# Six residual additions of a gated recurrent layer moved into accumulating transfers

## The chip, the cores and the metric

The kernel runs on one core of one Trainium2 chip. The metric is device microseconds of one execution. The kernel before took 118.81 us in the median of three runs (118.44 to 119.31). The execution under the profiler took 118.47 us, 0.34 us under that median.

## The reference, cut to what matters

```python
# inputs x: (16 sequences, 512 steps, 128 features), float32
xn = layernorm(x)
r, k, v = split(xn @ W_rkv + b_rkv, 3);  r = sigmoid(r);  k = exp(k);  kv = k * v
gamma = exp(nu_log + gamma_log) - 1;     lam = exp(-exp(nu_log))
u1, u2 = scan(lam, kv), scan(lam, k)          # y[t] = lam * y[t-1] + u[t] along the 512 steps
s = ((u1 + gamma * kv) / (u2 + gamma * k + 1e-6) * r) @ W_o + b_o
g = silu(fp6_quantised(xn) @ fp6_quantised(W_ffn).T + bias)   # blocks of 32, one scale each
out = x + s * g
```

The last line is the residual addition that the change is about.

## The kernel before, in words

A sequence is one tile of 128 partitions x 512 float32 elements (256 KB); there are 16, and all of them stay in `x_all`. Every sequence goes through the same stages, spread over the engines:

- VectorE: `statistics` of the layer norm, `block_maxima` and scales of the quantisation, `key_values` (k times v), the two scans `scan_den` and `scan_num`, `receive` (numerator times receptance), `gating` (projection times gate).
- GpSimd: a quarter of `normalise`, `quantise`, `dequantise`, `gamma_k`, `denominator` and `ratio` (the last six mostly for two sequences at once).
- ScalarE: three quarters of `normalise`, the copies of the turned tiles out of PSUM, exponential, tanh, silu, the logarithm and its inverse for the division, and the seven pairs of table loads between the set of exp and log and the set of silu and tanh (`exp_phase`, `silu_phase`).
- TensorE: transposes of `xn` and `xd`, the matmuls `keys`, `receptance`, `values`, `ffn`, `project`, and `untranspose` of the gated product.

The term gamma times kv of the numerator is added by TensorE (`gamma_kv`, a matmul with a diagonal matrix that accumulates in `num_ps`) for the eight even sequences, and by VectorE for the eight odd ones. The residual of sequence n is added in one of two ways. For the 12 sequences of `RES_DVE`, VectorE adds `x_all` and the PSUM bank `so_ps` into `x_all`. For the four of `RES_POOL`, 2, 5, 8 and 11, ScalarE copies the bank to one of two buffers `product` (`copy_out`, line 824), and GpSimd adds that to `x_all` (line 390). SyncE then stores `x_all[:, n, :]` to the output, 16 stores in order of sequence. `project(n + 1)` uses the same PSUM bank `so_ps` up to sequence 12, so it waits until the residual or the copy of n has read it.

The order of the work is written out by hand, one list for each engine, and each engine runs its list in order and stops at a semaphore that has not come. Two more lists, `TURNS` and `TAKEN`, give the order in which two pairs of PSUM banks are used: `turned_ps` (transposes, emptied by ScalarE's copies) and `taken_ps` (keys, receptance and ffn, emptied by ScalarE's exp, tanh and silu). The use i of a pair waits until use i - 2 has been emptied. `project(15)` takes the bank `taken_ps[0]` after all 48 uses, so it waits for `gates(15)` on ScalarE.

SyncE issues the 16 loads of x and the three weight loads first, and then the stores.

Of the kernel before, what the change touches and what calls it, by code (L numbers as in the profile page):

```python
# [5 lines left out]
def build(nc, x_in, w_rkv, b_rkv, w_o, b_o, nu_log, gamma_log, w_ffn, b_ffn, out):  # L6
# [10 lines left out]
    SEQS, L, D = x_in.shape  # L17
# [30 lines left out]
    def batch_of(batches, n):  # L48
# [3 lines left out]
    RES_POOL = [2, 5, 8, 11]  # L52
    RES_DVE = [n for n in range(SEQS) if n not in RES_POOL]
    STORES = [0, 1, 2, 3, 4, 5, 6, 7, 8, 9, 10, 11, 12, 13, 14, 15]
# [27 lines left out]
    with ctx:  # L82
# [34 lines left out]
        product = sb("product", [P, 2, W])  # L117
# [107 lines left out]
        pool_result = sem("pool_result")  # L225
# [43 lines left out]
        def _(sp):  # L269
# [10 lines left out]
            for n in range(4, SEQS):  # L280
                load(n)
            for n in STORES:
                if n in RES_POOL:
                    sp.wait_ge(pool_result, RES_POOL.index(n) + 1)
                else:
                    sp.wait_ge(dve_result, RES_DVE.index(n) + 1)
                sp.dma_start(out_v[:, n, :], x_all[:, n, :]).then_inc(stored, 16)
            sp.wait_ge(stored, SEQS * 16)

        @block.gpsimd  # L290
        def _(pool):
# [108 lines left out]
            normalise(2)  # L400
            dequantise(0)
            deviations(3)
            normalise(3)
            inv_std(3)
            quantise(1)
            gamma_k(0)
            normalise(4)
            denominator(0)
            gamma_k(1)
            dequantise(1)  # L410
            normalise(5)
            denominator(1)
            quantise(2, 2)
            dequantise(2, 2)
            normalise(6)
            deviations(4)
            ratio(0)
            normalise(7)
            inv_std(4)
            gamma_k(2, 2)  # L420
            quantise(4, 2)
            ratio(1)
            normalise(8)
            dequantise(4, 2)
            gamma_k(4, 2)
            denominator(2, 2)
            normalise(9)
            quantise(6, 2)
            normalise(10)
            denominator(4, 2)  # L430
            ratio(2, 2)
            deviations(5)
            dequantise(6, 2)
            inv_std(5)
            gamma_k(6, 2)
            residual(2)
            normalise(11)
            quantise(8, 2)
            ratio(4, 2)
            normalise(12)  # L440
            denominator(6, 2)
            dequantise(8, 2)
            normalise(13)
            quantise(10, 2)
            dequantise(10, 2)
            normalise(14)
            gamma_k(8, 2)
            ratio(6, 2)
            gamma_k(10, 2)
            residual(5)  # L450
            denominator(8, 2)
            denominator(10, 2)
            normalise(15)
            quantise(12, 2)
            ratio(8, 2)
            dequantise(12, 2)
            gamma_k(12, 2)
# [6 lines left out]
            gamma_k(14)  # L464
            gamma_k(15)
            denominator(14)
            denominator(15)
            dequantise(15)
            ratio(12, 2)
            ratio(14)  # L470
            ratio(15)
            residual(11)

        @block.vector
        def _(dve):
# [125 lines left out]
            out_weights()  # L601
            statistics(4)
            block_scales(0)
            inverse_scales(0)
            statistics(5)
            statistics(6)
            statistics(7)
            decay_column()
            key_values(0)
            scan_den(0)  # L610
            ffn_weights()
            block_maxima(1)
            gamma()
            block_scales(1)
            inverse_scales(1)
            scan_num(0)
            key_values(1)
            statistics(8)
            block_maxima(2)
            statistics(9)  # L620
            scan_den(1)
            block_scales(2)
            inverse_scales(2)
            block_maxima(3)
            key_values(2)
            statistics(10)
            receive(0)
            statistics(11)
            scan_num(1)
            block_scales(3)  # L630
            inverse_scales(3)
            gamma_kv(1)
            key_values(3)
            receive(1)
            scan_den(2)
            scan_num(2)
            gating(0)
            key_values(4)
            scan_den(3)
            residual(0)  # L640
            statistics(12)
            key_values(5)
            receive(2)
            block_maxima(4)
            statistics(13)
            statistics(14)
            scan_num(3)
            block_scales(4)
            inverse_scales(4)
            gamma_kv(3)  # L650
            gating(1)
            scan_den(4)
            scan_den(5)
            receive(3)
            key_values(6)
            residual(1)
            scan_num(4)
            statistics(15)
            key_values(7)
            block_maxima(5)  # L660
            receive(4)
            block_scales(5)
            inverse_scales(5)
            key_values(8)
            gating(2)
            scan_num(5)
            scan_den(6)
            gamma_kv(5)
            scan_den(7)
            gating(3)  # L670
            receive(5)
            key_values(9)
            scan_num(6)
            residual(3)
            block_maxima(6)
            receive(6)
            gating(4)
            scan_num(7)
            residual(4)
            block_scales(6)  # L680
            inverse_scales(6)
            gamma_kv(7)
            scan_den(8)
            scan_den(9)
# [3 lines left out]
            gating(5)  # L688
            block_maxima(7)
            receive(8)  # L690
            scan_den(10)
            scan_num(9)
            scan_den(11)
            gating(6)
            gamma_kv(9)
            key_values(11)
            receive(9)
            residual(6)
            scan_num(10)
            block_scales(7)  # L700
            inverse_scales(7)
            gating(7)
            scan_den(12)
            scan_den(13)
            key_values(12)
            residual(7)
            block_maxima(8)
            receive(10)
            gating(8)
            scan_num(11)  # L710
            block_scales(8)
            inverse_scales(8)
            gamma_kv(11)
            scan_den(14)
# [3 lines left out]
            key_values(13)  # L718
            scan_den(15)
            receive(12)  # L720
            residual(9)
            scan_num(13)
            key_values(14)
            gating(10)
            gamma_kv(13)
            receive(13)
            residual(10)
            scan_num(14)
            key_values(15)
            gating(11)  # L730
            receive(14)
            scan_num(15)
            gamma_kv(15)
            receive(15)
            gating(12)
            gating(13)
            gating(14)
            residual(12)
# [6 lines left out]
        def _(act):  # L745
# [510 lines left out]
```

## Time and profile before

| | |
|---|---|
| profiled execution | 118.47 us, span of the core 116.7 us |
| TensorE (PE) busy | 107.5 us, 92% of the span |
| VectorE (DVE) busy | 105.6 us, 91% |
| ScalarE (ACT) busy | 101.7 us, 87% |
| GpSimd (POOL) busy | 100.8 us, 86% |
| DMA | 8.81 MB, mean 76 GB/s |

A share is busy time over the span. The span holds a head in which the first tiles are loaded and normalised, and a tail of the last residual and its store, so no engine can reach 100%. Outside the span lie 1.77 us of the execution. Matmuls overlap their neighbours: the time from one to the next, in the chain of work, is shorter than the mean duration of one.

### The profile page before, as it was taken

Reading aid. Unit: us, or ns where it says so; the run is one execution under the profiler, and the core shown is the slowest. Engines: PE = TensorE matmul, PEld = TensorE weight load, DVE = VectorE, ACT = ScalarE, POOL = GpSimd, SP = SyncE. Lnnn points to the kernel's source line nnn. Section 1 sums busy time; section 2 is a strip of 40 time slices with the busy share of each in tenths; the row PEclk is TensorE's granted clock in tenths of the full one; section 3 lists DMA queues with packets and bytes.
Section 4 is the critical chain, followed back from the end, with each engine's and each line's share of the span. In section 5 each row is a group of like instructions: output and inputs, shape, how many; then the busy total and the mean of one; then the engine's idle time right before and its main releaser. Section 6 shows DMA issues by size and latency. Waiting matters only on the chain.

```text
span 116.7 us, 1669 instructions
## 1 busy us (share of the span) xinstructions
PE 107.5 (92%) x403; PEld 59.1 (51%) x403; DVE 105.6 (91%) x171; ACT 101.7 (87%) x176; POOL 100.8 (86%) x110
## 2 busy tenths in 40 slices
PE   4947999979999999999999999999999999999970
PEld 4934435535455546445473544755545554545550
DVE  0539999999999999999998999999999899999891
ACT  4049899999999999999999999999998999899700
POOL 2189978999999999798999999999999999997800
PEclk9999999999999999999999999999999999999996
DMA  2869960000002000200022100021111021020047
GB/s 70 244 199 404 386 248 0 0 6 3 6 0 90 0 0 0 90 0 0 18 77 90 65 25 0 0 89 43 53 41 54 0 90 72 18 90 0 0 184 265
DMA packets 6024, 8.81 MB, mean 76 GB/s; under 512 B 1536, under 2 KB 1920, under 8 KB 6016
## 3 DMA queue, kind: packets, MB, share of 16 engines
q1 hardware_dynamic: 5040, 8.72, 20.7%
q10 hardware_dynamic: 976, 0.00, 0.5%
q8 instruction: 3, 0.05, 0.2%
q14 instruction: 5, 0.04, 0.1%
HBM read 4.53 MB, written 4.19 MB: 75 GB/s over the span
## 4 chain that ended last, share of the span: by engine, by line
PE 74%; ACT 12%; DVE 3%; DMA 3%; POOL 3%; issue 1%; DVEq 1%; ACTq 0%; POOLq 0%
PE taken_ps L1020 32%; PE turned_ps L1001 11%; PE so_ps L1076 10%; PE v_ps L1048 10%; PE num_ps L1062 5%; PE so_ps L1082 5%; ACT xn L764 5%; DMA x_all<-in_L_attn_inputs_dram 3%; ACT L747 2%; POOL rstd L316 2%; ACT k L792 2%; ACT recept L799 2%; DVE x_all L553 2%; PE turned_ps L1076 1%; DVE gate L548 1%
## 5 line engine op out<-in xcount | busy, mean ns | idle before, releaser
L1020 PE MATMUL taken_ps<-xnT,wrkv_sb 128*128 128x512 f32 x64 | 31.8, 597 | 0.3 <-ACT k L792 0.3
L764 ACT ACTIVATE xn<-x_all,shift,rstd 128x128 f32<-128x128 f32 x48 | 20.1, 497 | 5.7 <-POOL shift L336 5.7
L384 POOL TENSOR_TENSOR mixed<-mixed,den 128x1024 f32<-128x1024 f32 (+1 forms) x10 | 19.3, 1934 | 2.0 <-ACT den L817 1.2
L527 DVE TENSOR_TENSOR_SCAN num_ps<-own_ps,kv 128x512 f32<-128x512 f32 x16 | 19.4, 1215 | 0.0
L378 POOL TENSOR_TENSOR den<-den,gk 128x1024 f32<-128x1024 f32 (+1 forms) x10 | 19.2, 1930 | 0.1
L517 DVE TENSOR_TENSOR_SCAN den<-own_ps,k 128x512 f32<-128x512 f32 x16 | 19.1, 1207 | 0.0
L747 ACT ACT_TABLE_LOAD x14 | 18.0, 1283 | 0.9 <-PEq L1243 0.7
L481 DVE BATCH_NORM_STATS2 stats<-x_all 128x6 f32<-128x256 f32 x32 | 11.7, 417 | 6.2 <-DMA x_all<-in_L_attn_inputs_dram 6.2
L1048 PE MATMUL v_ps<-xnT,wrkv_sb 128*128 128x512 f32 x32 | 16.4, 595 | 0.0
L1020 PE MATMUL taken_ps<-xdT,wdT 128*128 128x512 f32 x32 | 16.2, 599 | 0.1
L355 POOL TENSOR_TENSOR q<-xn,inv_scale 128x1024 fp8e4<-128x1024 f32 (+1 forms) x10 | 15.7, 1571 | 0.4 <-DVE inv_scale L500 0.4
L362 POOL TENSOR_TENSOR xd<-q,scale 128x1024 f32<-128x1024 fp8e4 (+1 forms) x10 | 15.7, 1568 | 0.3
L1020 PEld LDWEIGHTS taken_ps<-xnT,wrkv_sb 128*128 128x128 f32 x64 | 11.0, 190 | 9.5 <-issue 8.7
L1076 PE MATMUL so_ps<-mixed,wos_sb 128*128 128x512 f32 x26 | 13.8, 611 | 0.0
L1001 PEld LDWEIGHTS turned_ps<-ident,xn 128*128 128x128 f32 x64 | 7.5, 141 | 12.0 <-issue 9.6
L1001 PE MATMUL turned_ps<-ident,xn 128*128 128x128 f32 x64 | 9.8, 276 | 3.7 <-POOL xn L347 2.3
L508 DVE SCALAR_TENSOR_TENSOR kv<-v_ps,cols,k 128x512 f32<-128x512 f32 x16 | 11.7, 731 | 0.1
L807 ACT ACTIVATE gate<-taken_ps,cols 128x512 f32<-128x512 f32 x16 | 10.9, 695 | 0.6 <-PE taken_ps L1020 0.5
L792 ACT ACTIVATE k<-taken_ps,cols 128x512 f32<-128x512 f32 x16 | 10.9, 692 | 0.5 <-PE taken_ps L1020 0.4
L542 DVE SCALAR_TENSOR_TENSOR mixed<-recept,num_ps 128x512 f32<-128x512 f32 x16 | 10.8, 674 | 0.1
L799 ACT ACTIVATE recept<-taken_ps,half_br 128x512 f32<-128x512 f32 x16 | 10.8, 692 | 0.0
L548 DVE SCALAR_TENSOR_TENSOR gate<-so_ps,cols,gate 128x512 f32<-128x512 f32 x13 | 9.6, 741 | 1.1 <-ACT recept L799 0.5
(73 smaller groups left out, 188.2 us busy)
## 6 DMA issues: line engine op xcount, KB each, us to landing
x_all<-in_L_attn_inputs_dram SPq DMA_DIRECT2D x16, 256.0 KB, 6.6
out_dram<-x_all SPq DMA_DIRECT2D x16, 256.0 KB, 2.0
wrkv_sb<-in_L_attn_W_rkv_dram SPq DMA_DIRECT2D x1, 192.0 KB, 4.4
wf_sb<-in_L_ffn_weight_dram SPq DMA_DIRECT2D x1, 64.0 KB, 6.3
wo_sb<-in_L_attn_W_o_dram SPq DMA_DIRECT2D x1, 64.0 KB, 6.1
cols<-in_L_attn_nu_log_dram ACTq DMA_DIRECT2D x1, 0.5 KB, 3.8
cols<-in_L_attn_gamma_log_dram ACTq DMA_DIRECT2D x1, 0.5 KB, 4.0
cols<-in_L_attn_b_o_dram ACTq DMA_DIRECT2D x1, 0.5 KB, 4.6
```

The lines of the kernel that those rows point to most:

```text
L355: nc.gpsimd.tensor_tensor(blocks(ring(q, n, m)), blocks(ring(xn, n, m)), spread(iscale(n, m)), ALU.mult, saturate=False).then_inc(q_ready, m)
L362: nc.gpsimd.tensor_tensor(blocks(ring(xd, n, m)), blocks(ring(q, n, m)), spread(scale[:, n * BPS:(n + m) * BPS]), ALU.mult).then_inc(xd_re ...
L378: nc.gpsimd.tensor_tensor(ring(den, n, m), ring(den, n, m), ring(gk, n, m), ALU.add)\
L384: nc.gpsimd.tensor_tensor(ring(mixed, n, m), ring(mixed, n, m), ring(den, n, m), ALU.mult)\
L517: nc.vector.tensor_tensor_scan(den[:, n % DEN, :], lam_ps.to_broadcast([P, W]), k[:, n % KS, :], 0.0, ALU.mult, ALU.add).then_inc(den_scan ...
L527: nc.vector.tensor_tensor_scan(num_ps[:, :], lam_ps.to_broadcast([P, W]), kv[:, n % KS, :], 0.0, ALU.mult, ALU.add).then_inc(num_scanned, 1)
L747: act.add_instruction(mybir.InstLoadActFuncSet(name=nc.get_next_instruction_name(), engine=mybir.EngineType.Activation, act_func_set_id=n, ...
L764: ins = nc.scalar.activation(xn[:, n % XN, j * D:(j + 1) * D], x_all[:, n, j * D:(j + 1) * D], ACT.Identity, bias=shift[:, t:t + 1], scale ...
L1001: ins = nc.tensor.transpose(in_time(turned_ps[i % 2][:, :])[:, :, j], source[:, j * D:(j + 1) * D], ident[:, :])
L1020: nc.tensor.matmul(taken_ps[i % 2][:, :], weights, moving, start=True, stop=True).then_inc(filled, 1)
L1048: nc.tensor.matmul(v_ps[:, :], wrkv_sb[:, 2 * D:3 * D], xnT[:, n % XNT, :], start=True, stop=True)\
L1076: nc.tensor.matmul(SO_BANKS[n][:, :], wos_sb[:, :], mixed[:, n % MIX, :], start=True, stop=True)\
```

## The change

`RES_POOL` grows from four sequences to six: 2, 4, 6, 8, 10 and 12. Their rows of x are stored to the output before any residual (`placed`), by SyncE behind the loads. GpSimd no longer adds in SBUF: its `residual(n)` issues a transfer that adds `product` to the output in HBM. `product` has four buffers instead of two. `gamma_kv` goes to TensorE for ten sequences (0, 1, 3, 4, 6, 8, 10, 12, 14, 15) and stays on VectorE for six (2, 5, 7, 9, 11, 13). The lists of all engines are written out in a new order.

```diff
-    RES_POOL = [2, 5, 8, 11]
+    RES_POOL = [2, 4, 6, 8, 10, 12]
+    PRODUCTS = 4
     TURNS = [
-        ("xn", 0), ("xn", 1), ("xn", 2), ("xn", 3), ("xd", 0), ("xn", 4), ("xn", 5), ("xd", 1), ("xd", 2),
+        ("xn", 0), ("xn", 1), ("xn", 2), ("xd", 0), ("xn", 3), ("xn", 4), ("xn", 5), ("xd", 1), ("xd", 2),
...
-        product = sb("product", [P, 2, W])
+        product = sb("product", [P, PRODUCTS, W])
...
-        pool_result = sem("pool_result")
+        placed = {n: sem(f"placed{n}") for n in RES_POOL}
+        added = [sem(f"added{i}") for i in range(len(RES_POOL))]
...
             for n in range(4, SEQS):
                 load(n)
+            for n in RES_POOL:
+                sp.wait_ge(x_loaded[n], 16)
+                sp.dma_start(out_v[:, n, :], x_all[:, n, :]).then_inc(placed[n], 16)
             for n in STORES:
                 if n in RES_POOL:
-                    sp.wait_ge(pool_result, RES_POOL.index(n) + 1)
-                else:
-                    sp.wait_ge(dve_result, RES_DVE.index(n) + 1)
+                    continue
+                sp.wait_ge(dve_result, RES_DVE.index(n) + 1)
                 sp.dma_start(out_v[:, n, :], x_all[:, n, :]).then_inc(stored, 16)
-            sp.wait_ge(stored, SEQS * 16)
+            sp.wait_ge(stored, len(RES_DVE) * 16)
+            for done in added:
+                sp.wait_ge(done, 16)
...
             def residual(n):      # GpSimd
                 i = RES_POOL.index(n)
                 pool.wait_ge(copied_out, i + 1)
-                nc.gpsimd.tensor_tensor(x_all[:, n, :], x_all[:, n, :], product[:, i % 2, :], ALU.add)\
-                    .then_inc(pool_result, 1)
+                pool.wait_ge(placed[n], 16)
+                nc.gpsimd.dma_start(out_v[:, n, :], product[:, i % PRODUCTS, :], accum_op=ALU.add)\
+                    .then_inc(added[i], 16)
...
             def copy_out(n):      # ScalarE
                 i = RES_POOL.index(n)
                 act.wait_ge(o_done, n + 1)
-                if i >= 2:
-                    act.wait_ge(pool_result, i - 1)
-                nc.scalar.activation(product[:, i % 2, :], so_ps[:, :], ACT.Copy).then_inc(copied_out, 1)
+                if i >= PRODUCTS:
+                    act.wait_ge(added[i - PRODUCTS], 16)
+                nc.scalar.activation(product[:, i % PRODUCTS, :], so_ps[:, :], ACT.Copy).then_inc(copied_out, 1)
```

The new order at the start of TensorE's list, against the old one:

```
before: xn0 xn1 k0 v0 k1 xn2 arm r0 r1 v1 xn3 r2 xd0 v2 xn4 wd gkv0 k2 k3 xn5 v3 k4 k5 xd1 xd2 ffn0 r3 p0 v4 r4
        gkv2 un0 v5 xn6 ffn1 xn7 r5 xd3 p1
after:  xn0 xn1 k0 v0 k1 xn2 arm xd0 r0 v1 xn3 r1 gkv0 r2 k2 xn4 xn5 v2 k3 gkv1 k4 xd1 v3 k5 xd2 wd v4 p0
        ffn0 ffn1 v5 xd3 r3 un0 xn6 r4 p1
```

(xn, xd and wd are transposes, k, r, v, ffn and p the matmuls `keys`, `receptance`, `values`, `ffn` and `project`, gkv is `gamma_kv`, un is `untranspose`.) At the end, TensorE's list has `project(12)`, `gamma_kv(15)`, `project(13)`, `ffn(15)`, `untranspose(12)`, `project(14)`, `project(15)`, `untranspose(13)` to `untranspose(15)`. VectorE's ends with the gatings 13 to 15 and the residuals 13, 14 and 15; before, `residual(12)` stood ahead of `gating(15)`. ScalarE's list ends with `gates(14)`, `gates(15)` and `copy_out(12)`; the other five copies stand ahead of these, where before there were four.

## Rows read from the trace of the kernel before

**Rows 1.** The page: busy time of each engine, and the chain that ended last, by engine.
```profile
PE 107.5 (92%) x403; PEld 59.1 (51%) x403; DVE 105.6 (91%) x171; ACT 101.7 (87%) x176; POOL 100.8 (86%) x110
PE 74%; ACT 12%; DVE 3%; DMA 3%; POOL 3%; issue 1%; DVEq 1%; ACTq 0%; POOLq 0%
```

**Rows 2.** Busy time by stretch: stretch, its length, PE, PEld, DVE, ACT, POOL, clock, DMA share, GB/s.
```profile
9.00:25.00 16.00, 14.13 (x49) 6.82 (x49) 15.61 (x41) 15.44 (x34) 14.57 (x26) 1.00 0.49 184
25.00:110.00 85.00, 84.57 (x305) 44.58 (x306) 83.28 (x118) 83.49 (x139) 81.24 (x70) 1.00 0.09 35
```

**Rows 3.** The chain that ended last, in order of time: start us, us, what.
```profile
0.72 3.61 DMA x_all<-in_L_attn_inputs_dram
...
15.08 0.48 ACT xnT L773
...
25.06 0.63 PE turned_ps L1001 x4
...
33.83 0.86 PE num_ps L1062 x2
34.69 0.47 PE so_ps L1082 x4
...
36.02 0.44 PE turned_ps L1001 x4
...
39.06 0.86 PE so_ps L1076 x2
...
108.34 1.73 PE turned_ps L1076 x4
...
111.55 0.75 DVE gate L548
112.30 1.20 DVE x_all L553 x2
```

**Rows 4.** Waits, all engines: who waited for whom, us in total, times, longest.
```profile
PE turned_ps L1001 <- ACT xdT L780: 0.8, 1, 0.8
```

**Rows 5.** Groups of instructions, forms apart, of the lines that the change touches.
```profile
L1062 PE MATMUL num_ps<-kv,gam_diag 128*128 128x512 f32 x16 | 8.2, 593 | 0.0
L533 DVE SCALAR_TENSOR_TENSOR num_ps<-kv,gam,num_ps 128x512 f32<-128x512 f32 x8 | 5.7, 708 | 0.0
L553 DVE TENSOR_TENSOR x_all<-so_ps,x_all 128x512 f32<-128x512 f32 x9 | 6.1, 677 | 0.0
L390 POOL TENSOR_TENSOR x_all<-x_all,product 128x512 f32<-128x512 f32 x4 | 5.1, 1284 | 0.0
L824 ACT ACTIVATE product<-so_ps 128x512 f32<-128x512 f32 x4 | 2.4, 594 | 0.5 <-PE so_ps L1082 0.5
```

**Rows 6.** The same view: groups that bound the cost of an issue on GpSimd.
```profile
L384 POOL TENSOR_TENSOR mixed<-mixed,den 128x1024 f32<-128x1024 f32 x6 | 14.2, 2373 | 0.9 <-ACT den L817 0.6 <-issue 0.2
L316 POOL TENSOR_TENSOR rstd<-var,minus_half 128x4 f32<-128x4 f32 x2 | 2.0, 1024 | 0.0
L500 DVE RECIPROCAL inv_scale<-scale 128x32 f32<-128x32 f32 x7 | 2.5, 353 | 0.2
```

**Rows 7.** Timeline of the ramp: start us, us, engine, line, instruction, count.
```profile
13.29 0.75 DVE L508 SCALAR_TENSOR_TENSOR kv<-v_ps,cols,k 128x512 f32<-128x512 f32 x1
13.73 1.05 POOL L362 TENSOR_TENSOR xd<-q,scale 128x512 f32<-128x512 fp8e4 x1
17.56 1.02 PE L1048 MATMUL v_ps<-xnT,wrkv_sb 128*128 128x512 f32 x2
22.44 1.28 ACT L747 ACT_TABLE_LOAD   x1
26.70 1.91 POOL L362 TENSOR_TENSOR xd<-q,scale 128x1024 f32<-128x1024 fp8e4 x1
```

**Rows 8.** SyncE's queue: the last loads, the stores by line, and their time to landing.
```profile
4.00 6.80 SPq L271 DMA_DIRECT2D x_all<-in_L_attn_inputs_dram  x12
L287 SPq DMA_DIRECT2D out_dram<-x_all x16: 332/332/347, 36.1 to 114.1; - x16
out_dram<-x_all SPq DMA_DIRECT2D x16, 256.0 KB, 2.0
```

**Rows 9.** Timeline of the tail.
```profile
108.93 1.27 ACT L807 ACTIVATE gate<-taken_ps,cols 128x512 f32<-128x512 f32 x2
109.70 1.29 POOL L390 TENSOR_TENSOR x_all<-x_all,product 128x512 f32<-128x512 f32 x1
110.37 1.07 PE L1076 MATMUL taken_ps<-mixed,wos_sb 128*128 128x512 f32 x2
```

More of the change, by code:

```diff
@@ L400, in _ @@
             normalise(2)
+            normalise(3)
+            deviations(3)
             dequantise(0)
-            deviations(3)
-            normalise(3)
+            gamma_k(0)
+            gamma_k(1)
             inv_std(3)
             quantise(1)
-            gamma_k(0)
+            denominator(0)
             normalise(4)
-            denominator(0)
-            gamma_k(1)
+            normalise(5)
             dequantise(1)
-            normalise(5)
-            denominator(1)
             quantise(2, 2)
-            dequantise(2, 2)
             normalise(6)
             deviations(4)
+            denominator(1)
+            dequantise(2, 2)
             ratio(0)
+            inv_std(4)
+            quantise(4, 2)
             normalise(7)
-            inv_std(4)
-            gamma_k(2, 2)
-            quantise(4, 2)
             ratio(1)
@@ L428, in _ @@
             quantise(6, 2)
+            dequantise(6, 2)
             normalise(10)
             denominator(4, 2)
+            gamma_k(6, 2)
+            normalise(11)
+            deviations(5)
             ratio(2, 2)
-            deviations(5)
-            dequantise(6, 2)
             inv_std(5)
-            gamma_k(6, 2)
+            quantise(8, 2)
+            gamma_k(8, 2)
             residual(2)
-            normalise(11)
-            quantise(8, 2)
-            ratio(4, 2)
             normalise(12)
             denominator(6, 2)
+            normalise(13)
+            ratio(4, 2)
             dequantise(8, 2)
-            normalise(13)
+            denominator(8, 2)
             quantise(10, 2)
-            dequantise(10, 2)
[L446 to L451, printed above, removed]
+            residual(4)
+            normalise(14)
+            normalise(15)
+            gamma_k(10, 2)
+            ratio(6, 2)
+            dequantise(10, 2)
             denominator(10, 2)
-            normalise(15)
+            gamma_k(12, 2)
+            residual(6)
+            ratio(8, 2)
             quantise(12, 2)
-            ratio(8, 2)
             dequantise(12, 2)
-            gamma_k(12, 2)
             denominator(12, 2)
@@ L464, in _ @@
             gamma_k(14)
+            dequantise(15)
             gamma_k(15)
+            residual(10)
             denominator(14)
+            ratio(12, 2)
             denominator(15)
-            dequantise(15)
-            ratio(12, 2)
             ratio(14)
             ratio(15)
-            residual(11)
+            residual(12)
         @block.vector
@@ L641, in _ @@
+            block_maxima(4)
+            gating(1)
+            gamma_kv(2)
             statistics(12)
-            key_values(5)
             receive(2)
-            block_maxima(4)
+            residual(1)
+            block_scales(4)
+            inverse_scales(4)
+            scan_num(3)
+            scan_den(4)
+            key_values(6)
+            scan_den(5)
+            receive(3)
+            key_values(7)
+            scan_num(4)
             statistics(13)
             statistics(14)
-            scan_num(3)
@@ L648, in _ @@
[L648 to L657, printed above, removed]
             statistics(15)
-            key_values(7)
+            key_values(8)
+            receive(4)
             block_maxima(5)
-            receive(4)
+            scan_num(5)
             block_scales(5)
             inverse_scales(5)
-            key_values(8)
+            gamma_kv(5)
@@ L992, in _ @@
             gates(15)
+            copy_out(12)
         @block.tensor
@@ L1111, in _ @@
-            values(3)
-            keys(4)
-            keys(5)
-            transpose_xd(1)
-            transpose_xd(2)
+            keys(3)
+            gamma_kv(1)
+            keys(4)
+            transpose_xd(1)
+            values(3)
+            keys(5)
+            transpose_xd(2)
+            transpose_wd()
+            values(4)
+            project(0)
             ffn(0)
+            ffn(1)
+            values(5)
+            transpose_xd(3)
             receptance(3)
-            project(0)
@@ L1119, in _ @@
-            values(4)
+            untranspose(0)
+            transpose_xn(6)
             receptance(4)
-            gamma_kv(2)
-            untranspose(0)
-            values(5)
-            transpose_xn(6)
-            ffn(1)
+            project(1)
             transpose_xn(7)
             receptance(5)
-            transpose_xd(3)
-            project(1)
-            transpose_xn(8)
-            ffn(2)
-            ffn(3)
-            values(6)
-            transpose_xn(9)
-            keys(6)
@@ L1136, in _ @@
-            keys(7)
+            receptance(6)
             untranspose(1)
             transpose_xd(4)
+            keys(6)
+            values(6)
+            transpose_xd(5)
+            keys(7)
+            transpose_xn(8)
+            gamma_kv(3)
+            values(7)
+            transpose_xn(9)
             keys(8)
-            values(7)
+            transpose_xd(6)
             keys(9)
+            values(8)
             gamma_kv(4)
-            transpose_xd(5)
-            values(8)
+            ffn(2)
@@ L1158, in _ @@
             transpose_xn(11)
             gamma_kv(6)
-            project(4)
             ffn(6)
             transpose_xn(12)
-            untranspose(4)
+            receptance(10)
+            project(4)
+            transpose_xn(13)
             keys(10)
```

295 lines of the change are left out of this document (145 added, 150 removed), and 12 rows, old and new, of tables (TAKEN, TURNS).

## The prediction

> **What bounds the kernel now.** I read the busy shares first, then the chain that ended last, then the stretches. The shares alone don't decide: four engines stand between 86% and 92% [rows 1]. The chain does. It lies on TensorE for 74% of the span [rows 1], and in order of time it stays there from the transpose at 25.06 us to the end of `project(14)` at 108.34 + 1.73 = 110.07 us [rows 3]. The stretch 25 to 110 us says how close the others come: of 85.0 us TensorE is busy 84.6, ScalarE 83.5, VectorE 83.3 and GpSimd 81.2 [rows 2]. So GpSimd has 3.8 us to spare there and no other engine more than 1.7; TensorE ends last, but nobody is far behind it.
>
> TensorE's busy time hides a little waiting, since a matmul's record is longer than its step. Its steps in the chain are 0.86 us for a matmul of 512 columns in its two passes, 0.44 for four transposes of xn or xd, 0.47 for an untranspose [rows 3]. Between 25.06 and 110.07 us its list has 76 such matmuls, 26 transposed tiles and 12 untransposed ones: 65.4 + 11.4 + 5.6 = 82.4 us of 85.0. So 2.6 us of waits are left in it.
>
> The tail is tied to two engines. `gates(15)` ends at 108.93 + 1.27 = 110.20 us, and `project(15)`, which needs its bank, starts at 110.37 [rows 9]; then come its gating, its untranspose, the residuals 14 and 15 and a store of 2.0 us [rows 3, 8].
>
> **The change part by part.**
>
> *TensorE* gets two more `gamma_kv`, at 0.86 us from one to the next [rows 3]; the 593 ns of a pass overlap [rows 5]. That is +1.72 us on the engine that is the chain. What could cover it is its 2.6 us of waits and the ramp.
>
> *The ramp.* Before, `xn5` waits 0.8 us for ScalarE to copy xd0, whose bank it takes over [rows 4]; it starts at 25.06 [rows 3]. In the new `TURNS`, xd0 comes ahead of xn3, so xn4 and xn5 take over banks long empty. I walk the four new lists by hand with the steps of the old trace, and note where TensorE would stop. xd0 on GpSimd moves behind a normalise and two small instructions, from 13.73 to 14.8, so its 1.05 us end near 15.85 [rows 7]; TensorE waits some 0.5 us for it. The product kv of sequence 0 on VectorE (13.29 before [rows 7]) moves behind block maxima, gamma and scales to about 15.4, and values(1) is then due at 17.2, against 17.56 before [rows 7]. xn4 and xn5 follow at 21.9 and 22.3, keys(3) ends at 24.5, gamma_kv(1) at 25.5 behind its scan. xd2 waits about 0.5 us for a dequantise on GpSimd which, at 26.70 before [rows 7], now stands behind a quantise, a normalise, the deviations and a denominator and ends near 29.0. `project(0)` is then due at 30.5 and `project(1)` at 36.95 to 37.8. Before, project(1) ended at 39.06 + 0.86 = 39.92 [rows 3]. The new list has by then left out receptance(5) and one transpose, 0.86 + 0.44 = 1.3 us: equal work is done at 39.1, so TensorE is 0.8 us ahead, both extra `gamma_kv` not yet paid in full. (gamma_kv(2) of before is matched by gamma_kv(1); the two extra ones come later, 3 beside 4, and 15.) On the same walk ScalarE is not ahead: its table load at 22.44 [rows 7] moves 0.48 later for the copy of xd0 that now stands ahead of it.
>
> *ScalarE* gets two more copies out. A copy is 594 ns alone and 0.48 from start to start in a row [rows 3, 5]. One lies ahead of `gates(15)`: +0.5 us with 0.1 from the ramp, +0.6. The other lies after it, covered by the tail's work on TensorE and VectorE. ScalarE has 1.5 us free [rows 2], so this is less than TensorE's term and beside it.
>
> *VectorE* loses two `gamma_kv` and two residuals: 2 x 708 + 2 x 677 ns = 2.8 us [rows 5]. It isn't the chain before the tail, so nothing of that comes off the sum directly. In the tail `residual(12)` no longer stands ahead of `gating(15)`, but that one waited for project(15) just as long (110.37 + 1.07 = 111.44 against a start at 111.55 [rows 3, 9]): -0.1.
>
> *GpSimd* loses four additions, 5.1 us in all [rows 5], 4.1 of them ahead of 110 us, since the last starts at 109.70 [rows 9]. It gets six issues, five of them ahead of 110 us. The trace has no transfer issued by GpSimd. The cost c of an issue is bounded below by SyncE's issue of the same tile, 0.33 us [rows 8], and above by the longest instruction that GpSimd runs, 2.37 [rows 6]. I take 1.0: this is software on GpSimd over few operands, and the nearest row is the power of 4 elements per partition, 1.02 us though it moves almost nothing [rows 6]. Then GpSimd's stretch is 81.2 - 4.1 + 5.0 = 82.1 us of 85: almost no relief, no harm. Range: 78.8 to 89.0.
>
> The Trainium skill, DMA: Bandwidth & Descriptors, section Latency and other measured facts, puts the first byte of a GpSimd-issued transfer at about 1 us and lays it on the descriptors being written by its cores; as an estimate of c that leaves the sum where it is, and no run here shows it yet. One of its rules speaks against the change: by SBUF — State Buffer, section Who interferes with whom, VectorE in a two-port mode locks GpSimd out of writing descriptors. VectorE's small SBUF-only instructions here last up to 353 ns [rows 6], so by that rule six issues would cost at most 2.1 us more, on an engine with 2.9 us left.
>
> Queued behind each issue on GpSimd are the next quantise, ratio or normalise, for whom TensorE and ScalarE wait; that is how c would show. Its wait for `placed` costs nothing: the stores ahead go out behind the loads.
>
> *SyncE* issues six more stores at 0.33 us [rows 8]. They wait for x behind the last load's issue at 4.00 + 6.80 = 10.8 us [rows 8], in the same queue as the loads, and the first ordinary store is at 36.1 [rows 8]. So I cost them at nothing: the queue's order keeps them behind the loads, and DMA is 9% busy after 25 us [rows 2]. Without that cover, 1.5 MB at the ramp's 184 GB/s [rows 2] would be 8 us of DMA, and the statistics of the last sequences would be late next.
>
> *Sum:* +1.72 - 0.8 - 0.1 = +0.8 us on a span of 116.7, so 117.5, and 119.3 us for that execution (118.47 before). The median stands 0.34 us above the profiled one (118.81), so I forecast 119.6 us.
>
> **The rivals.**
>
> *A, the relief closes TensorE's waits.* VectorE is 2.8 us freer, and GpSimd too if c is near its lower bound. If TensorE's 2.6 us of waits came from them being late, the re-ordered lists could take these away: +0.8 - 2.6 = -1.8, span 114.9, time 117.0; with a little of it left, 117.2. For it: both are within 4 us of full, and the buffers are short. Against: ScalarE is as full and gets more work, so it can't go far under +0.6 less its own 1.5 us of idle, -0.9, unless its records too hide waits, as TensorE's do.
>
> *B, GpSimd becomes the bound (slower).* Its place is the stretch 25 to 110 us. 81.2 - 4.1 + 5c passes 85 from c = 1.6 on, if GpSimd never waits. At c = 2.0 it is 87.1; with half of its former idle time, 1.9, kept, 89.0. That is +2.1 to +4.0 us, about +3.1: 121.9 us. For it: GpSimd does everything in software (1.28 us for a tile that VectorE adds in 0.68 [rows 5]). Against: an issue touches no elements.
>
> *C, the last accumulating transfer lands last.* copy_out(12) ends near 110.2 + 0.6 = 110.8, the issue at 111.8, both 0.8 later with the shift. Landing is bounded by a store, 2.0 us [rows 8], and by a read and a store, 3.6 + 2.0 = 5.6 [rows 3, 8], as it must read the output first; I take 3.5. SyncE's last store goes out at 114.1 and lands at 116.1 [rows 8], so the transfer decides from a landing of 4.3 us on. At 5.6 it adds 1.3: 120.9 us.
>
> *D, the change doesn't relieve anybody.* If c is about 1.28, the issue costs what the addition did. That is inside the forecast: +0.8 either way.
>
> **How the numbers follow.** What a measurement can tell from no change is about 1%, 1.2 us: under 117.6 is faster, over 120.0 slower. The forecast gets 0.45, from 118.9 to 120.5; 0.35 of this lies within 1%, 0.10 over it. A gets 0.29, 0.25 of it faster. B gets 0.18, 0.16 of it slower. C gets 0.08, half and half between within and slower. That makes faster 0.25, within 0.45, slower 0.30. The range goes from A at 117.2 to B at 121.9 us; outside are A with every wait gone, and c near 2.37.
>
> **What would show it.** TensorE: the wait for xdT at 25 us gone, project(1) ending at 37.8, and the chain on TensorE from about 25 to 111 us. GpSimd: the gap around each residual's issue gives c; under 0.6 speaks for A, over 1.6 for B. The tail: last landing by SyncE's store of 15, else C. ScalarE starting `gates(15)` before 109.5 would refute my sum, and so would waits on GpSimd's issues as the cause of idle TensorE; a chain that leaves TensorE for ScalarE or VectorE in the middle of the span would mean that the two extra matmuls were not the price.

## The result and the profile after

The changed kernel took 121.75 us in the median of four runs (121.68 to 122.1), beside 118.66 us for the kernel before (118.44 to 119.31). The ratio is 1.026, with a 95% interval of 1.023 to 1.030: 3.1 us slower. The forecast was 119.6 us and no measurable change. The time lies inside the range of 117.2 to 121.9 us only because that range was wide; it comes near the 121.9 us of rival B, and not for that rival's reason, as the experiments show.

The changed kernel's page, with busy time by engine and the chain that ended last by engine, answers to [rows 1]:

```profile
PE 109.7 (92%) x407; PEld 60.1 (50%) x407; DVE 106.3 (89%) x167; ACT 102.9 (86%) x178; POOL 101.1 (84%) x112
PE 69%; DVE 17%; DMA 5%; issue 4%; SPq 1%; DVEq 1%
```

VectorE lost two `gamma_kv` and two residuals, four instructions in all, and yet it is busy 0.7 us longer; and it holds 17% of the chain where it held 3%. Its busy time by stretch, in the columns of [rows 2]:

```profile
9.00:25.00 16.00, 14.58 (x53) 7.41 (x54) 15.75 (x40) 15.36 (x33) 14.92 (x27) 1.00 0.75 282
25.00:110.00 85.00, 83.67 (x302) 43.58 (x301) 83.44 (x115) 82.18 (x139) 80.12 (x70) 1.00 0.17 38
```

TensorE, nearly full before (84.57 of 85.00), is idle for 1.3 us here. The chain in order of time says where: it runs on VectorE up to 31.3 us, and on TensorE from there (before, from 25.06).

```profile
25.88 0.65 DVE kv L518
26.52 0.20 DVE wmax L586
26.73 0.02 issue
26.75 0.59 DVE wscale L589
...
27.58 1.75 DVE wq L594
...
30.53 0.75 DVE kv L518
31.28 0.14 issue
31.41 1.10 PE v_ps L1056 x2
...
39.04 0.86 PE so_ps L1084 x2
```

The span is cut at two matmuls of `project`: `project(1)`, the last row above, at 39.04 us in the chain (39.06 before [rows 3]), and `project(15)`, at 112.53 in the rows below (110.37 before [rows 9]). A timeline gives the same `project(1)` a start 0.17 us earlier than the chain does, 38.87 and 38.89, so the two measures are not mixed below. The changed kernel's tail, by TensorE, GpSimd and SyncE's queue:

```profile
112.53 1.09 PE L1084 MATMUL taken_ps<-mixed,wos_sb 128*128 128x512 f32 x2
...
113.17 0.88 POOL L398 DMA_DIRECT2D out_dram<-product  x1 [1.37 <-ACT product L830]
...
115.10 1.53 SPq L292 DMA_DIRECT2D out_dram<-x_all  x3
```

| stretch | before | after | difference |
|---|---|---|---|
| to `project(1)`; the new list has then left out 1.3 us of TensorE's work | 39.06 | 39.04 (and 1.3) | +1.3 |
| `project(1)` to `project(15)`, less that 1.3 | 71.3 | 73.5 - 1.3 | +0.9 |
| `project(15)` to the end of the span | 6.3 | 7.3 | +0.9 |

The sum is the 3.1 us between the spans, 116.7 and 119.8.

How the transfers themselves look is seen in two rows on the line that issues them, and in the DMA part of the page:

```profile
L398 POOL DMA_DIRECT2D out_dram<-product x6: 877/884/1145, 60.0 to 113.2; - x6
DMA to landing us min/median/max: 3.7/4.0/4.4
```

```profile
out_dram<-x_all SPq DMA_DIRECT2D x16, 256.0 KB, 3.1
out_dram<-product POOLq DMA_DIRECT2D x6, 256.0 KB, 4.0
```

The 3.1 us is a median over three kinds of store: the six beforehand, beside the loads (7.4 us in the median), the seven of the body (2.0), and the last three, which are the matter of the tail below (3.1).

An issue is recorded with 0.88 us. GpSimd's timeline shows that less than that is lost, since the next instruction starts before the record ends:

```profile
92.91 0.88 POOL L398 DMA_DIRECT2D out_dram<-product  x1
93.52 1.35 POOL L362 TENSOR_TENSOR q<-xn,inv_scale 128x512 fp8e4<-128x512 f32 x1
```

From start to start it is 0.61 us here. The other four ahead of the last have 0.64, 0.64, 0.67 and 0.85. An addition in SBUF had 1.24 (75.90 to 77.14 us in the trace of before).

GpSimd's busy time misleads here. Behind the first issue most of its other records are some 0.3 us longer and overlap the next one, though the steps are the old ones:

```profile
61.28 2.66 POOL L385 TENSOR_TENSOR den<-den,gk 128x1024 f32<-128x1024 f32 x1
63.64 0.72 POOL L354 TENSOR_SCALAR xn<-x_all,rstd,shift 128x128 f32<-128x128 f32 x1
```

The denominator is recorded with 2.66 us (2.37 before), but the next instruction starts 2.36 us after it.

### The profile page after: what moved, and what is told of

Its sections match the earlier page's. It is cut to its first block, busy times and chain, and to the rows that moved or that the text cites. A ratio compares the mean times of both kernels' runs of the same rounds, so it can differ in the third digit from the quotient of the medians.

```text
span 119.8 us, 1686 instructions
## 1 busy us (share of the span) xinstructions
PE 109.7 (92%) x407; PEld 60.1 (50%) x407; DVE 106.3 (89%) x167; ACT 102.9 (86%) x178; POOL 101.1 (84%) x112
## 4 chain that ended last, share of the span: by engine, by line
PE 69%; DVE 17%; DMA 5%; issue 4%; SPq 1%; DVEq 1%
PE taken_ps L1028 28%; PE so_ps L1084 10%; PE v_ps L1056 9%; PE turned_ps L1009 8%; PE num_ps L1070 6%; PE so_ps L1090 5%; DMA x_all<-in_L_attn_inputs_dram 5%; DVE stats L491 5%; DVE own_ps L498 2%; DVE den L527 2%; DVE kv L518 2%; DVE wq L594 1%; PE turned_ps L1084 1%; DVE num_ps L537 1%; SPq L273 1%
## 5 line engine op out<-in xcount | busy, mean ns | idle before, releaser
L391 POOL TENSOR_TENSOR mixed<-mixed,den 128x1024 f32<-128x1024 f32 (+1 forms) x10 | 20.8, 2080 | 1.0 <-DVE mixed L552 0.6
L385 POOL TENSOR_TENSOR den<-den,gk 128x1024 f32<-128x1024 f32 (+1 forms) x10 | 20.7, 2070 | 0.1
L362 POOL TENSOR_TENSOR q<-xn,inv_scale 128x1024 fp8e4<-128x1024 f32 (+1 forms) x10 | 16.5, 1646 | 1.8 <-issue 1.8
L369 POOL TENSOR_TENSOR xd<-q,scale 128x1024 f32<-128x1024 fp8e4 (+1 forms) x10 | 16.8, 1677 | 0.3
L1009 PEld LDWEIGHTS turned_ps<-ident,xd 128*128 128x128 f32 x64 | 7.7, 142 | 6.3 <-issue 4.2
```

Of the source, the lines that this page charges most:

```text
L369: nc.gpsimd.tensor_tensor(blocks(ring(xd, n, m)), blocks(ring(q, n, m)), spread(scale[:, n * BPS:(n + m) * BPS]), ALU.mult).then_inc(xd_re ...
L385: nc.gpsimd.tensor_tensor(ring(den, n, m), ring(den, n, m), ring(gk, n, m), ALU.add)\
L391: nc.gpsimd.tensor_tensor(ring(mixed, n, m), ring(mixed, n, m), ring(den, n, m), ALU.mult)\
L1009: ins = nc.tensor.transpose(in_time(turned_ps[i % 2][:, :])[:, :, j], source[:, j * D:(j + 1) * D], ident[:, :])
```

## The experiments

Medians differ by some tenths between the chips, so each kernel is compared by its ratio to the kernel before on the same chip; a difference of 0.001 in a ratio is about 0.12 us.

**The ffn weight's scales in PSUM.** On the chain above stand instructions of a group of five small ones that quantise the ffn weight: a maximum, a scale (`wscale`), its reciprocal, and two products (`wq`, `wd`). Side by side, VectorE and GpSimd of the changed kernel between 25 and 31 us:

```profile
26.75 0.58 DVE L589 TENSOR_SCALAR wscale<-wmax 128x4 f32<-128x4 f32 x1
27.37 0.18 DVE L592 RECIPROCAL wiscale<-wscale 128x4 f32<-128x4 f32 x1
27.58 1.74 DVE L594 TENSOR_TENSOR wq<-wf_sb,wiscale 128x128 fp8e4<-128x128 f32 x1
29.36 1.25 DVE L597 TENSOR_TENSOR wd<-wq,wscale 128x128 f32<-128x128 fp8e4 x1
...
26.03 1.28 POOL L385 TENSOR_TENSOR den<-den,gk 128x512 f32<-128x512 f32 x1
27.27 1.91 POOL L369 TENSOR_TENSOR xd<-q,scale 128x1024 f32<-128x1024 fp8e4 x1
29.14 1.32 POOL L391 TENSOR_TENSOR mixed<-mixed,den 128x512 f32<-128x512 f32 x1
```

The ends are what to look at: 27.33 against 27.31, 29.32 against 29.18, 30.61 against 30.46. Each of the three ends just after the GpSimd instruction that was running. The reciprocal, which runs inside GpSimd's dequantise as well, keeps its 0.18 us. In the kernel before, the same work stood beside GpSimd instructions of 0.2 to 0.5 us:

```profile
15.39 0.17 DVE L579 TENSOR_SCALAR wscale<-wmax 128x4 f32<-128x4 f32 x1
15.81 0.29 DVE L584 TENSOR_TENSOR wq<-wf_sb,wiscale 128x128 fp8e4<-128x128 f32 x1
16.13 0.29 DVE L587 TENSOR_TENSOR wd<-wq,wscale 128x128 f32<-128x128 fp8e4 x1
```

The edit takes no work away. It moves the input and the output of wscale and of the reciprocal, and one input of each product, from SBUF to PSUM:

```diff
-        wmax = sb("wmax", [P, BPW])
-        wscale = sb("wscale", [P, BPW])
-        wiscale = sb("wiscale", [P, BPW])
+        wmax, wscale, wiscale = (own_ps[:, at:at + BPW] for at in (400, 408, 416))
```

> The changed kernel with one edit: the three small columns of the ffn weight's quantisation (wmax, wscale, wiscale) lie in a free part of the PSUM bank own_ps instead of SBUF, so VectorE's five instructions on that weight read SBUF through at most one operand. No list is reordered. Theory P (port collision): in the changed kernel wscale, wq and wd take 0.58, 1.74 and 1.25 us instead of 0.17, 0.29 and 0.29, and each ends within 0.1 us of the end of a GpSimd instruction; with one operand in PSUM they take under 0.5 us each, kv of sequence 3 comes about 2.5 us earlier, project(0) starts near 30.5 instead of 32.35, and the time falls by about 1.9 us, from 121.75 to 119.9 us (ratio to before 1.010). Rival O (order alone): the chain is late because of where it stands in the list, the long records are its waits; then the time stays at 121.4 to 121.8 us (ratio 1.024).

Measured: 119.92 us, ratio 1.011 (1.006 to 1.016). VectorE's timeline of that kernel, the same instructions in the same place, while the same GpSimd product runs (27.20 to 29.12 us):

```profile
26.69 0.17 DVE L587 TENSOR_SCALAR own_ps<-own_ps 128x4 f32<-128x4 f32 x1
26.90 0.19 DVE L590 RECIPROCAL own_ps<-own_ps 128x4 f32<-128x4 f32 x1
27.12 0.29 DVE L592 TENSOR_TENSOR wq<-wf_sb,own_ps 128x128 fp8e4<-128x128 f32 x1
27.45 0.29 DVE L595 TENSOR_TENSOR wd<-wq,own_ps 128x128 f32<-128x128 fp8e4 x1
```

and TensorE's `project(1)`:

```profile
37.13 1.02 PE L1082 MATMUL so_ps<-mixed,wos_sb 128*128 128x512 f32 x2
```

The stretch is gone and 1.8 us of the 3.1 are back. `project(1)` starts 1.74 us earlier than in the changed kernel; in the chain's measure, which the prediction's walk used, it is at 37.30 us where the walk had 36.95. The order was mostly not what failed; the durations were. The new order also moves the scaling of the output weight, from 10.05 to 24.10 us. It takes 0.65 us there instead of 0.21 and ends 0.09 us after a quantise on GpSimd; here, with input and output still in SBUF, it takes 0.49.

**One part of the new order in the kernel before.** The same weight work moved late in the old lists, with the scales in SBUF and then in PSUM.

```diff
 # VectorE                          # TensorE                     # ScalarE
             scan_den(0)
-            ffn_weights()
...
             key_values(2)
+            ffn_weights()
...
             transpose_xd(2)
+            transpose_wd()         # was ahead of gamma_kv(0)
...
             keys(5)
             inverse(1)
+            copy_wdT()             # was behind keys(3)
```

> The kernel before with one part of the new order alone: VectorE quantises the ffn weight behind key_values(2), near 25.4 us, where GpSimd runs additions and products of two operands in SBUF, instead of near 15 us, where it runs small ones. The transpose of the weight and its copy move behind transpose_xd(2) and inverse(1). Theory P (port collision): wscale, wq and wd together take at least 1.5 us more than the 0.75 us they take before, and the kernel gets 1 to 2 us slower, 119.5 to 120.5 us (ratio 1.009 to 1.017). Rival O (order alone): the five instructions keep their 1.3 us in all, 118.3 to 118.9 us.

> e8_before_late_weights, with wmax, wscale and wiscale in PSUM as in e1. The same order of work, without a second SBUF operand on VectorE. Theory P: no stretched instruction, 118.3 to 118.9 us (ratio 0.998 to 1.003). Rival O: the same as e8, whatever that is.

Measured: 122.05 us, ratio 1.024 (1.017 to 1.032) with the scales in SBUF; 119.78 us, ratio 1.006 (1.002 to 1.011) in PSUM. The first is slower than expected, the second slightly too, so the late place costs 0.7 us by itself and the collision 2.2 us on top. In the first, by VectorE and then GpSimd:

```profile
25.24 0.89 DVE L579 TENSOR_SCALAR wscale<-wmax 128x4 f32<-128x4 f32 x1
26.16 0.18 DVE L582 RECIPROCAL wiscale<-wscale 128x4 f32<-128x4 f32 x1
26.38 1.93 DVE L584 TENSOR_TENSOR wq<-wf_sb,wiscale 128x128 fp8e4<-128x128 f32 x1
...
24.19 1.91 POOL L355 TENSOR_TENSOR q<-xn,inv_scale 128x1024 fp8e4<-128x1024 f32 x1
26.25 1.91 POOL L362 TENSOR_TENSOR xd<-q,scale 128x1024 f32<-128x1024 fp8e4 x1
```

wscale (4 elements per partition) ends at 26.13, GpSimd's quantise at 26.10; wq ends at 28.31, the dequantise at 28.16. The reciprocal again takes its 0.18 us. This is the collision made in a kernel that had none.

**The weights early, in SBUF.** The practical way round: back to a place where GpSimd runs small instructions.

```diff
             block_maxima(0)
+            out_weights()
...
             scan_den(0)
+            ffn_weights()
             statistics(9)
```

> The changed kernel with VectorE's two pieces of weight work back near their old places, and still in SBUF: out_weights behind block_maxima(0), ffn_weights behind scan_den(0), near 17.2 us, where GpSimd runs only small instructions. Theory P: the five instructions take about 1.3 us in all, scan_num(0) and gamma_kv(0) come 1.3 us later and cost TensorE up to 0.9 us there, the 2.3 us of waits at 28.5 to 31.4 go: 1.0 to 1.9 us less than the changed kernel, ratio 1.011 to 1.018. Rival O (what counts is not the port but something else behind the weights in the list): 1.022 or over.

Measured: 120.97 us, ratio 1.017 (1.013 to 1.021), the slow end of the expectation. wscale, wq and wd take 0.22, 0.29 and 0.29 us. `scan_num(0)` comes later, and TensorE waits 0.95 us for it ahead of `gamma_kv(0)`, at 20.56 us. By the ratios this brings 1.1 us where the scales in PSUM brought 1.8, and `project(1)` starts 1.2 us later than with these: the place costs some of what it avoids.

**The tail.** The last accumulating transfer, of sequence 12, is issued at 113.17 us. It has landed before the last store, at 117.5, but its packets, 0.18 us each for 2 KB where a store's take 0.09, move until 117.15. The last three stores are issued from 115.10 on, and their first packet starts 1.4 us later, where a store alone has 0.8. The last of them is issued at 116.30 and waited for until 119.4: 3.1 us, against 2.2 before. Two edits on top of the scales in PSUM: the residual of 12 given to VectorE, and, in a second kernel, given to GpSimd as an addition in SBUF.

```diff
 # given to VectorE
-    RES_POOL = [2, 4, 6, 8, 10, 12]
+    RES_POOL = [2, 4, 6, 8, 10]
...
             gating(14)
+            residual(12)
             gating(15)
 # or added in SBUF by GpSimd, stored ahead of 13
+                if n == RES_POOL[-1]:
+                    nc.gpsimd.tensor_tensor(x_all[:, n, :], x_all[:, n, :], product[:, i % PRODUCTS, :], ALU.add)\
+                        .then_inc(last_added, 1)
+                    return
```

> e1_psum_scales with one more edit: the residual of sequence 12 is added by VectorE again (ahead of gating 15, as before) and stored by SyncE; five accumulating transfers are left. Theory L (the accumulating transfer of 12 runs beside the last three stores and stretches the last one: 3.1 us from issue to the end of SyncE's wait instead of 2.2): the stretch from project(15) to the end falls from 7.1 to about 6.3 us, so 119.1 us (ratio 1.003), against 119.9 for e1. Rival N (that stretch is longer for another reason, such as the longer list of semaphores at the end, or VectorE's extra residual takes it back): 119.7 us or more.

> e1_psum_scales with the residual of sequence 12 added in SBUF by GpSimd and stored by SyncE ahead of 13; the other five stay accumulating transfers, no list of a compute engine is changed and VectorE gets nothing more. Theory L (the accumulating transfer in the tail stretches the last stores): from project(15) to the end 6.3 to 6.5 us as in the kernel before, instead of 7.1, so 0.6 to 0.8 us less than e1, ratio to before 1.004 (e1: 1.011). Rival N (the tail is longer for the semaphores that SyncE waits on, or for another reason): the same tail and time as e1, ratio 1.010.

Measured: 120.01 us, ratio 1.009 (1.005 to 1.012) for the first; 119.49 us, ratio 1.004 (1.001 to 1.007) for the second, as forecast. In the second, `project(15)` starts at 111.79 and the span ends at 118.2: 6.4 us, as before. SyncE's queue and the landings of that kernel:

```profile
113.53 2.37 SPq L294 DMA_DIRECT2D out_dram<-x_all  x4
```

```profile
out_dram<-x_all SPq DMA_DIRECT2D x16, 256.0 KB, 2.1
```

The last store takes 2.2 us again. So theory L holds, worth 0.7 us in the trace (a tail of 7.1 us with the scales alone, 6.4 here) and 0.8 by the ratios (1.011 to 1.004), whose intervals just overlap. The first edit brought 0.2 us at most, which its interval cannot tell from nothing: VectorE's extra residual stands ahead of `gating(15)`, and the load of TensorE's weights for `untranspose(15)` waits 0.5 us for that gating.

**The mechanism alone.** The kernel before, its lists untouched, with the four residuals sent as accumulating transfers.

```diff
-                nc.gpsimd.tensor_tensor(x_all[:, n, :], x_all[:, n, :], product[:, i % 2, :], ALU.add)\
-                    .then_inc(pool_result, 1)
+                pool.wait_ge(placed[n], 16)
+                nc.gpsimd.dma_start(out_v[:, n, :], product[:, i, :], accum_op=ALU.add).then_inc(added[i], 16)
```

> The kernel before with the mechanism alone: residuals 2, 5, 8 and 11 go out as accumulating transfers onto x stored beforehand, four product buffers; no list is reordered and VectorE keeps its twelve residuals. Theory M: an issue holds GpSimd for 0.61 to 0.85 us from its start to the next instruction, against 1.24 for the addition, so GpSimd gains 4 x 0.6 = 2.4 us, but TensorE is the chain; the last transfer is issued near 109.7 and lands near 114.5, ahead of the last store. So 118.2 to 118.9 us (ratio 0.996 to 1.002). Rival R (the relief is what TensorE waits for): 117.5 us or less. Rival C (accumulating transfers are slow and are waited for): 119.5 us or more.

Measured: 119.05 us, ratio 1.004 (1.001 to 1.008), just over the band of theory M; the profiled execution has the span of before, 116.7. By stretch, the kernel before and then this one (40 to 110 us):

```profile
40.00:110.00 70.00, 69.63 (x251) 36.73 (x250) 68.32 (x93) 68.61 (x109) 66.94 (x53) 1.00 0.10 38
```

```profile
40.00:110.00 70.00, 69.69 (x252) 36.74 (x250) 68.32 (x93) 68.52 (x108) 65.90 (x53) 1.00 0.16 38
```

GpSimd is 1.0 us less busy (66.94 to 65.90), and from start to start three issues take 2.2 us where three additions took 3.7; TensorE gains nothing. Rival A's reading of GpSimd's relief is refuted for this order of work. The last three stores take 2.4 us here against 2.1, which may be the excess over the band; that was not tried apart.

**The mechanism taken out of the changed kernel.** Six additions in SBUF, everything else as changed.

```diff
-                pool.wait_ge(placed[n], 16)
-                nc.gpsimd.dma_start(out_v[:, n, :], product[:, i % PRODUCTS, :], accum_op=ALU.add)\
-                    .then_inc(added[i], 16)
+                nc.gpsimd.tensor_tensor(x_all[:, n, :], x_all[:, n, :], product[:, i % PRODUCTS, :], ALU.add)\
+                    .then_inc(pool_result, 1)
```

> The changed kernel, its lists and its six sequences, but the residuals are added in SBUF by GpSimd again and stored by SyncE; no stores beforehand, four product buffers kept. GpSimd gets 6 x 0.6 = 3.6 us more, the tail loses the late accumulating transfer (0.7 us of waiting at the end in the changed kernel). If GpSimd has that much room: 121.0 us (ratio 1.020). If GpSimd becomes the bound: 122.5 us or more (ratio over 1.032), and then the transfers do bring something in this order of work.

Measured: 121.44 us, ratio 1.025 (1.019 to 1.030), the same as with the transfers. From project(1) to project(15) it takes 113.51 - 39.77 = 73.74 us by the timeline, against 112.53 - 38.87 = 73.66 with transfers. So the transfers neither cost nor bring anything in the body of this kernel, and rival B is refuted: five additions take 2.8 us more there than the five issues, and GpSimd is still not the bound. The tail is no shorter, 7.0 us: this kernel stores 12 behind 13 and 14, right ahead of 15, and the last store takes 2.6 us beside them. The stores beforehand are gone here too, so this does not tell them from the transfers.

**`gamma_kv` given back to VectorE.** Three kernels were tried: 3 and 15 in the changed kernel; 12, behind scan_den(14), on top of the edits of scales and residual 12; and 12 behind residual(9), on top of the last addition in SBUF.

```diff
 # VectorE (and the same calls taken from TensorE's list)
             scan_num(3)
+            gamma_kv(3)
...
             gating(12)
+            gamma_kv(15)
 # second kernel                     # third kernel
             scan_den(14)                         residual(9)
+            gamma_kv(12)             +            gamma_kv(12)
             residual(9)                          scan_den(15)
```

> The changed kernel with gamma_kv 3 and 15 taken from TensorE and given to VectorE, as eight and eight stood before; nothing else. Theory T (TensorE is the rigid chain after the ramp): two matmuls of 0.86 us less, so 1.2 to 1.7 us faster, 120.0 to 120.5 us (ratio 1.011 to 1.016). Rival V (VectorE is as close): its 2 x 0.6 us more eat the gain, 121.3 us or more (ratio over 1.022).

> e5_scales_res12 with gamma_kv 12 moved from TensorE to VectorE, behind scan_den(14), in the stretch where VectorE idles 1.4 of 20 us. If TensorE is the rigid chain once no list starves it: 0.86 us less than e5, 118.2 us (ratio 0.996). If VectorE is as close there as it was for sequences 3 and 15: no less than e5, 119.1 us or more.

> e7_last_on_chip with gamma_kv 12 on VectorE, but behind residual(9) instead of ahead of it. In e6 it stood ahead and TensorE waited 0.9 us at project(10), which needs the bank that residual(9) frees. Theory T (TensorE is the chain, and loses a wait only where VectorE's list has no room): no such wait, 0.86 us less than e7, ratio 0.997. Rival V (VectorE is as close everywhere): some other wait appears and the time is that of e7 or more, ratio 1.004 or over.

Measured: 122.36 us, ratio 1.031 (1.026 to 1.036); 120.24 us, ratio 1.010 (1.005 to 1.016); 120.25 us, ratio 1.011 (1.007 to 1.015). Each is slower than its base or no faster (1.026, 1.009 and 1.004), though TensorE has one or two matmuls fewer. TensorE's timeline shows a new wait in each (in the first kernel also one of 0.85 us ahead of `project(15)`, for `gates(15)`). By kernel:

```profile
47.85 1.10 PE L1058 MATMUL v_ps<-xnT,wrkv_sb 128*128 128x512 f32 x2 [1.47 <-DVE kv L518]
```

```profile
97.62 1.10 PE L1082 MATMUL so_ps<-mixed,wos_sb 128*128 128x512 f32 x2 [0.73 <-DVE x_all L560]
```

```profile
99.53 0.75 PE L1097 MATMUL so_ps<-ident,gate 128*128 128x128 f32 x4 [0.55 <-DVE gate L564]
```

A 0.7 us instruction more on VectorE makes the next kv, residual or gating late, and TensorE waits for it. TensorE is the chain, but with VectorE one instruction behind it. Nor is VectorE alone: in the second and third kernel the chain runs back from that wait over VectorE to GpSimd's ratio, 2.7 us, which starts at 93.4 and 93.1. Theory T fell three times; rival V holds in all the places tried.

**The new bank order in the kernel before.** Two entries of `TURNS` swapped.

```diff
-        ("xn", 0), ("xn", 1), ("xn", 2), ("xn", 3), ("xd", 0), ("xn", 4), ("xn", 5), ("xd", 1), ("xd", 2),
+        ("xn", 0), ("xn", 1), ("xn", 2), ("xd", 0), ("xn", 3), ("xn", 4), ("xn", 5), ("xd", 1), ("xd", 2),
```

> The kernel before with one part of the new order alone: xd0 takes its turned bank ahead of xn3 (two entries of TURNS swapped, transpose_xd(0) ahead of transpose_xn(3) on TensorE, copy_xdT(0) ahead of copy_xnT(3) on ScalarE); residuals, gamma_kv and all the rest as before. Theory W (the 0.8 us for which xn5 waits at 24.3 us was TensorE's loss in the ramp, as the prediction has it): 0.5 to 0.8 us faster, ratio 0.993 to 0.996. Rival K (the next thing is late at the same time: values(3) needs kv of sequence 2, which VectorE ends at 25.4 us): within 0.2 us of before, ratio 0.999 to 1.002, and the wait stands ahead of values(3) instead.

Measured: ratio 1.000 (0.996 to 1.004). xn5 is transposed a microsecond earlier, and the wait stands ahead of values(3). TensorE's timeline:

```profile
24.05 0.60 PE L1001 MATMUL turned_ps<-ident,xn 128*128 128x128 f32 x4
25.81 1.10 PE L1048 MATMUL v_ps<-xnT,wrkv_sb 128*128 128x512 f32 x2 [1.17 <-DVE kv L508]
```

No kernel tried beats the one before. In the traces of the kernels with residual 12 on VectorE, with `gamma_kv` 12 behind scan_den(14), with the last addition in SBUF, and with late weights in PSUM, the granted clock stood at 0.50, the lower of its two levels (1.2 GHz), for some two to three us between 9 and 15 us, and `project(1)` comes up to 0.7 us later there (37.84 against 37.13 us with the same ramp); nothing above rests on those times, only on differences within one trace and on ratios.

## Why the prediction was wrong

*What bounds the kernel* held for the two kernels compared: TensorE carries the chain after the ramp in both, and full GpSimd was not the bound. Where the lists were changed further it did not always hold: with late weights in the old order the chain stays on VectorE to about 50 us, and with a `gamma_kv` given back it leaves TensorE in the middle of the span.

*The ramp* is the step that failed: -0.8 us forecast, +1.3 measured. Beside it, the tail was mis-sized (-0.1 against +0.9) and the two matmuls cost less than their term (+1.72 against +0.9 for the whole stretch). Together that is the 3.1 us measured against the +0.8 of the sum. The walk through the lists used each instruction's duration from the old trace. Three of them, 0.17, 0.29 and 0.29 us there, stood beside small GpSimd instructions, and the new order puts them beside GpSimd's long ones, of 1.3 to 1.9 us. They take 0.58, 1.74 and 1.25 us. That is 2.8 us more on VectorE, ahead of the kv that TensorE's values(4) waits for, and 1.8 us of the result. With the collision removed, the walk's project(1) is met within 0.35 us, and the ramp is 0.5 us ahead of before where the walk had 0.8. The Trainium skill states the rule, in SBUF — State Buffer, section Who interferes with whom: a VectorE instruction with two operands in SBUF contends with a GpSimd instruction that reads SBUF, and one in a two-port mode locks or is locked out for a whole instruction. The traces here agree: wq and wd, with two operands in SBUF, end with GpSimd's instruction, and the reciprocal, with one, is not held up (0.18 us). wscale has one operand in SBUF and was held up (0.58 us), which the rule allows in a two-port mode only; no run shows its mode. The prediction cited that very section, but asked only whether VectorE would hold up GpSimd's issues, and never what the new neighbours do to VectorE.

*The wait of xn5* was a wrong credit too: the isolated swap moved that wait to the next matmul and gained nothing. The prediction took a removed wait as time won without naming what is late next.

*TensorE's two matmuls*, +1.72 us, stand on the engine that holds the chain, but no run isolates their price: where one or two were given back, VectorE made TensorE wait instead. From project(1) to project(15) the changed kernel is 0.9 us longer, so some of the old waits did close. What is left once collision and tail are repaired, ratio 1.004, is +0.5 us, close to the forecast's +0.8. Which part of the new order gives that half of 1.72 back was not isolated.

*GpSimd's issue* was taken at 1.0 us and costs 0.6 to 0.85. It didn't matter, as the prediction said: six additions in SBUF take the same time.

*The tail* was forecast at -0.1 and came to +0.9. Landing was guessed at 3.5 us and is 3.7 to 4.4. Rival C had the place right and the mechanism half: the transfer is not the last to land, it slows the last store. That its price is near, 0.7 to 0.9 us where C had 1.3 at a landing of 5.6, is chance.

*ScalarE and SyncE* were not contradicted: no wait of TensorE points to a copy out. The stores placed beforehand were not tried apart from the transfers.

## What to carry to other kernels

Durations of an old trace hold only beside the old neighbours: before costing a re-ordered list, mark the VectorE instructions with two operands in SBUF, and scalings from SBUF to SBUF, even those of 4 elements, and see what GpSimd runs at their new place, or put the small operand in PSUM. A removed wait is worth nothing until the next operand is shown to be ready. A late transfer can lengthen the end without being last, if it still moves when the last stores are issued.

## What the runs showed that was not expected

A VectorE instruction on 128x4 elements took 0.89 us instead of 0.17, and one on 128x128 took 1.93 instead of 0.29, each ending within 0.15 us of the GpSimd instruction beside it; a reciprocal of 128x4 beside the same GpSimd work kept its 0.18 us. A GpSimd-issued accumulating transfer of 256 KB is recorded with 0.88 us, takes 0.61 to 0.85 from start to start, and lands 3.7 to 4.4 us after its issue, against 2.0 for SyncE's store of the same size in the body of the kernel. Its 2 KB packets take 0.18 us each, a store's 0.09.
